# Carrying a linear-attention state on every 64 tokens, in two visits a tile, instead of every 128

## What is computed

```python
def step(carry, inp):
    kv, ksum = carry
    kt, vt, qt = inp
    kv = kv + jnp.einsum('bhd,bhe->bhde', kt, vt)
    ksum = ksum + kt
    num = jnp.einsum('bhd,bhde->bhe', qt, kv)
    den = jnp.einsum('bhd,bhd->bh', qt, ksum)[..., None] + EPS
    return ((kv, ksum), num / den)
```

## Time and profile before

| | us |
|---|---|
| median of 3 runs | 1939.35 |
| lowest and highest | 1937.93 to 1939.39 |
| the profiled execution | 1939.27 |
| span of its trace | 1937.6 |
| PE busy | 1904.0 (98%) |
| DVE busy | 1586.2 (82%) |
| POOL busy | 891.4 (46%) |
| ACT busy | 664.3 (34%) |

### The profile page before, as it was taken

One profiled execution on the slowest core, in us unless ns is written; L12 is line 12 of the kernel. 1 busy time (PEld: TensorE's weight loads), 2 busy tenths in 40 slices (PEclk: granted clock), 3 DMA queues, 4 the chain that ended last, 5 costly groups with the idle time before them and its releaser, 6 DMA issues. The chain is left out here.

```text
span 1937.6 us, 60626 instructions
## 1 busy us (share of the span) xinstructions
PE 1904.0 (98%) x25412; PEld 1671.4 (86%) x25412; DVE 1586.2 (82%) x3379; ACT 664.3 (34%) x1297; POOL 891.4 (46%) x979
## 2 busy tenths in 40 slices
PE   7999999999999999999999999999999999999997
PEld 6788888888888888888888888888888888888886
DVE  6878878887879888778878987887788897878787
ACT  4333333333333233333333333333332333323331
POOL 4355443455443554534554445545345544355422
PEclk9999999999999999999999999999999999999998
DMA  6343234433343432333423334323433334333222
GB/s 202 94 133 106 92 111 125 127 110 104 100 127 110 128 118 74 127 121 115 122 99 105 116 111 138 113 85 111 132 116 116 98 96 129 113 126 119 75 72 84
DMA packets 171202, 218.03 MB, mean 113 GB/s; under 512 B 24369, under 2 KB 85809, under 8 KB 170929
## 3 DMA queue, kind: packets, MB, share of 16 engines
q1 hardware_dynamic: 168528, 213.59, 34.7%
q10 hardware_dynamic: 2400, 0.55, 0.1%
HBM read 151.02 MB, written 63.04 MB: 110 GB/s over the span
## 5 line engine op out<-in xcount | busy, mean ns | idle before, releaser
L1258 POOL TENSOR_TENSOR k_sum<-k_sum,q_raw 128x512 f32<-128x512 f32 x128 | 165.0, 1290 | 556.2 <-DVE q_raw L933 556.2
L836 ACT ACTIVATE e_tmp<-ring,bias_n 128x512 f32<-128x512 f32 x256 | 176.1, 688 | 509.9 <-PE ring L651 506.8
L922 DVE TENSOR_TENSOR s_mask<-ring,causal 128x512 f32<-128x512 f32 x512 | 314.9, 678 | 0.0
L669 PE MATMUL ring<-wv_hi,xt_hi 128*128 128x260 f32 x1024 | 299.3, 292 | 0.0
L669 PE MATMUL ring<-wo_hi,o_hi 128*128 128x260 f32 x1024 | 287.8, 282 | 1.2 <-ACT o_hi L886 1.0
L669 PE MATMUL ring<-wv_lo,xt_hi 128*128 128x260 f32 x1024 | 288.8, 282 | 0.0
L669 PE MATMUL ring<-wv_hi,xt_lo 128*128 128x260 f32 x1024 | 288.8, 282 | 0.0
L669 PE MATMUL ring<-wo_lo,o_hi 128*128 128x260 f32 x1024 | 288.4, 282 | 0.0
L669 PE MATMUL ring<-wo_hi,o_lo 128*128 128x260 f32 x1024 | 287.3, 284 | 0.9 <-DVE o_lo L1170 0.9
L886 ACT ACTIVATE o_hi<-num_ps 128x512 fp32r<-128x512 f32 x128 | 76.4, 597 | 475.0 <-PE num_ps L750 474.9
L651 PE MATMUL ring<-xt_hi,wk_hi 128*128 128x512 f32 x512 | 207.9, 406 | 5.2 <-DVE xt_lo L998 3.2
(11 more groups left out here) (140 smaller groups left out, 4060.3 us busy)
## 6 DMA issues: line engine op xcount, KB each, us to landing
x_tok<-in_x SPq DMA_DIRECT2D x128, 256.0 KB, 3.7
res<-in_x SPq DMA_DIRECT2D x128, 256.0 KB, 2.8
out<-res SPq DMA_DIRECT2D x128, 256.0 KB, 2.1
x_in<-in_x_t SPq DMA_DIRECT2D x124, 256.0 KB, 4.6
keys_turned<-k_turned SPq DMA_DIRECT2D x112, 256.0 KB, 2.0
k_tok<-keys_turned SPq DMA_DIRECT2D x448, 64.0 KB, 2.0
x_rows<-moments_rows SPq DMA_DIRECT2D x31, 512.0 KB, 3.7
k_t<-in_wk_t SPq DMA_DIRECT2D x4, 256.0 KB, 8.3
```

Source lines behind the costliest of these rows:

```text
L669: mm = pe.matmul(bank[:, 0:HW], rows[a](k), w[b][:, k, h, :], start=n == 0, stop=n == 3 * KD - 1)
L836: act.activation(e_tmp[:, m], bank, ACT.Relu, bias=bias_n[:, m, g:g + 1], scale=-1.0).then_inc(phi_relu.handle, 1)
L922: dve.tensor_tensor(s_mask[:, j], ring[:, st.bank(u)].rearrange("p (g t) -> p g t", g=KD), repeat(causal, KD), ALU.mult).then_inc(free[st. ...
L1258: pool.tensor_tensor(k_sum[:, g], k_sum[:, g], q_raw[:, g], ALU.mult).then_inc(prod.handle, 1)
```

## The change

A tile is now cut into two halves of 64 tokens (`HT`, `s` = 0 and 1), and the state is carried on after each half.

- **Scores** are computed only inside a half: 64 by 64 for each head and half. The two halves of the keys go to the two halves of the partitions of the same bank, so a bank now holds 256 columns. There are 32 products a tile in place of 16, on parts of 32 rows by 64 columns. The mask and `s_mask` are half as large, and so is each masking instruction of VectorE.
- **The state** is multiplied with the queries of each half (`from_state`, 16 products with 64 columns, twice a tile), and `add_state` adds the keys and values of each half (contraction over 64 rows, 16 products, twice a tile). The two halves use columns in different banks of `num_ps`. `sum_state` on VectorE and `keep_state` on ScalarE run twice a tile.
- **Two visits.** The first half's state work (`early_half`: `from_state` and `add_state`) is done at the end of the tile before, behind its output projection O; the second half's (`late_half`) stands where the state work stood.
- **Values in two goes.** The masked scores times values is done in `from_own_rows`, heads of the first bank on rows 0 to 63 and of the second bank on rows 64 to 127, and, behind the scores of the next tile (in tile 2 behind the denominators), in `from_other_rows` with the banks crossed. So no two row halves write one bank at a time. ScalarE's `o_hi` waits for the second go.
- The last tile of a sequence needs its keys too now, because its first half feeds its second; there are 128 turns of keys where there were 112. The first `early_half` of a block's tile 0 also waits for the values of tile 0.

The core of the diff:

```diff
-    KEY_TILES = [(b, c) for b in range(n_blocks) for c in range(TPB) if b % 2 == 0 or c < TPB - 1]
+    KEY_TILES = [(b, c) for b in range(n_blocks) for c in range(TPB)]
...
-    kv_ps = num_ps[:, 0, 2 * P:2 * P + KD * HD]
+    kv_ps = [num_ps[:, n, 2 * P:2 * P + KD * HD] for n in range(2)]
...
             for g in range(KD):
                 if c == 0:
                     pe.wait_ge(free[BANK[("R", g)]].handle, st.freed(("R", g)))
-                for j, u in enumerate(scores_of(c)):
-                    rows = slice(j * HD, (j + 1) * HD)
-                    mm = pe.matmul(ring[:, st.bank(u), g * P:(g + 1) * P], k_t[rows, par, g, t], q_div[rows, par, g, t],
-                                   start=True, stop=True, skip_group_check=True, tile_position=(j * HD, 0))
+                for s in range(2):
+                    t = slice(c * P + s * HT, c * P + (s + 1) * HT)
+                    for j, u in enumerate(scores_of(c)):
+                        rows = slice(j * HD, (j + 1) * HD)
+                        mm = pe.matmul(ring[s * HT:(s + 1) * HT, st.bank(u), g * HT:(g + 1) * HT],
+                                       k_t[rows, par, g, t], q_div[rows, par, g, t], start=True, stop=True,
+                                       skip_group_check=True, tile_position=(j * HD, s * HT))
...
+        def from_state(off, c, s):
...
+            pe.wait_ge(kv_kept.handle, kv_kept.at(HPG * n))
+            begins = (0, 1) if s == 0 else (1,) if first_of_pair(off, c, 0) else ()
             for g, j in HEADS_OF_PASSES:
+                r = j // 2
+                rows, t = slice(r * HT, (r + 1) * HT), slice(c * P + s * HT, c * P + (s + 1) * HT)
+                out, col = num_at(g, j, s)
+                pe.matmul(out, kv_diag[rows, g, j * HD:(j + 1) * HD], q_div[rows, off % 2, g, t],
+                          start=r in begins and g < 2, stop=r != s, skip_group_check=True, tile_position=(r * HT, col))
+
+        def add_state(off, c, s):
...
+            n = KEY_TILES.index((off, c))
+            pe.wait_ge(keys_in[n % 2].handle, 16 * HPG * (n // 2 + 1))
+            rows = slice(s * HT, (s + 1) * HT)
...
+        def products(c, crossed, done):
+
+            for four in range(0, HEADS, HPG):
+                r = four // HPG % 2
+                s = 1 - r if crossed else r
+                rows = slice(s * HT, (s + 1) * HT)
+                for g, j in HEADS_OF_PASSES[four:four + HPG]:
+                    head = (g * HPG + j) * HD
+                    out, col = num_at(g, j, s)
+                    mm = pe.matmul(out, v_tok[rows, c, head:head + HD], s_mask[rows, j, g], start=False, stop=True,
+                                   skip_group_check=True, tile_position=(s * HT, col))
+                if four >= HEADS // 2:
+                    mm.then_inc(done.handle, 1)
...
+        def from_other_rows(st, c):
+
+            pe.wait_ge(own_summed.handle, own_summed.at(2 * st.lin(TPB, st.off, c + 1)))
+            products(c, True, summed)
+
+        def early_half(st, off, c):
+
+            pe.wait_ge(o_lo.handle, o_lo.at(TPB * off + c))
+            if c == 0:
+                before = st if off > st.off else st.prev
+                for h in range(2):
+                    u = ("V", (0, h))
+                    pe.wait_ge(free[BANK[u]].handle, before.freed(u))
+            from_state(off, c, 0)
+            add_state(off, c, 0)
...
                 if attn:
-                    from_state(st, c)
-                    add_state(st, c)
-                    from_tile(st, c)
+                    late_half(st, c)
...
                     two_halves(st, "O", c, [lambda k, h=h: o_t[h][:, k, :] for h in range(2)], w_o)
+                    if not st.alone():
+                        early_half(st, *tile_after(st.off, c))
                 if c == 2 and proj:
                     spread_reciprocals(st)
...
                 if attn:
                     residual(st, c)
+                    if proj:
+                        sum_state(*tile_after(st.off, c), 0)
```

More of the change, by code:

```diff
@@ L18 @@
 KD = D // P
+HT = P // 2
 HPG = P // HD
@@ L727, in from_state @@
-        def from_state(st, c):
-            pe.wait_ge(o_lo.handle, o_lo.at(st.lin(TPB, st.off, c)))
-            if first_tile(st, c):
+                for s in range(2):
+                    t = slice(c * P + s * HT, c * P + (s + 1) * HT)
[4 more added lines that the diff above has]
+                                       skip_group_check=True, tile_position=(j * HD, s * HT))
+                        if g == KD - 1 and s == 1:
+                            mm.then_inc(full[st.bank(u)].handle, 1)
@@ L740, in from_tile @@
-        def from_tile(st, c):
+                r = j // 2
[4 more added lines that the diff above has]
+        def add_state(off, c, s):
+            if last_of_pair(off, c, s):
+                return
+            n = KEY_TILES.index((off, c))
+            pe.wait_ge(keys_in[n % 2].handle, 16 * HPG * (n // 2 + 1))
+            rows = slice(s * HT, (s + 1) * HT)
+            for g in range(KD):
+                for j in range(HPG):
+                    cols = slice((g * HPG + j) * HD, (g * HPG + j + 1) * HD)
+                    mm = pe.matmul(kv_ps[s][j * HD:(j + 1) * HD, g * HD:(g + 1) * HD], k_tok[rows, n % 2, j, g],
+                                   v_tok[rows, c, cols], start=first_of_pair(off, c, s) and g == 0, stop=True,
+                                   skip_group_check=True, tile_position=(s * HT, j * HD))
+            if s == 0:
+                mm.then_inc(kv_added.handle, 1)
@@ L746, in from_tile, with late_half @@
                     pe.wait_ge(free[BANK[u]].handle, st.before(BANK[u]) + CREDIT)
[L747 to L765 removed]
+            products(c, False, own_summed)
+        def from_other_rows(st, c):
[10 more added lines that the diff above has]
+            add_state(off, c, 0)
+        def late_half(st, c):
+            if c == 0:
+                for k in banks_of("V"):
+                    pe.wait_ge(free[k].handle, free[k].at(st.before(k)))
+            from_state(st.off, c, 1)
+            add_state(st.off, c, 1)
+            from_own_rows(st, c)
         def body(st):
@@ L780, in body @@
                         pe.wait_ge(xt_lo.handle, xt_lo.at(TPB * (st.off + 1)))
-                    chunks(st, c, 0, 1)
-                if attn:
-                    if c == 0 and st.off == 0:
-                        pe.wait_ge(ready["wo_t"].handle, READY["wo_t"])
-                    if c == 0:
-                        for k in banks_of("V"):
-                            pe.wait_ge(free[k].handle, free[k].at(st.before(k)))
-                    from_state(st, c)
-                    add_state(st, c)
-                    from_tile(st, c)
+                    chunks(st, c, 0)
+                    if attn and starts_late(st.off, c):
+                        pe.wait_ge(ready["wo_t"].handle, READY["wo_t"])
+                        early_half(st, st.off, c)
+                    chunks(st, c, 1)
+                if attn:
+                    late_half(st, c)
                 if c == 1 and not attn:
@@ L800, in body @@
                     scores(st, st.off + 1, 0)
+                if attn and (c != 2 or not proj):
+                    from_other_rows(st, c)
                 if proj:
@@ L805, in body @@
                 if attn:
+                    if st.alone() and not last:
+                        early_half(st, st.off, c + 1)
                     if st.alone():
@@ L871, in body @@
                 last = c == TPB - 1
+                if attn and not starts_late(st.off, c):
+                    keep_state(st.off, c, 0)
                 if c == 0 and proj:
@@ L1154, in body @@
                 if proj:
-                    chunks(st, c, 0, 1)
+                    chunks(st, c, 0)
+                    if attn and starts_late(st.off, c):
+                        sum_state(st.off, c, 0)
+                    chunks(st, c, 1)
                 if c == 0 and not attn:
@@ L1202, in body @@
                     choose(4, range(13, 17))
+                if st.alone() and not last:
+                    sum_state(st.off, c + 1, 0)
                 if attn:
                     residual(st, c)
+                    if proj:
+                        sum_state(*tile_after(st.off, c), 0)
                     if c != 2 or not proj:
```

125 lines of the change are left out of this document (58 added, 67 removed).

## The result

The changed kernel takes **2204.31 us** in the median (2191.31 to 2207.82, 4 runs), the kernel before 1939.37 us beside it (1937.93 to 1942.03): a ratio of 1.135, with a 95% interval from 1.130 to 1.140. The direction was forecast, the size was not: +265 us where +15 stood, far outside 1931 to 1990. The profiled execution has a span of 2206.1 us.

What follows compares the result with a forecast made beforehand. TensorE's own stream, busy 98% of the span, was taken as the bound. 1939.3 - 17 (stages) + 28 and 5 (keys) + 2 (masked bank) - 5 (shorter masks) + 2 (last block) = 1954 us, range 1931 to 1990.

Steps and rivals of the forecast that it cites:

- rival 4: TensorE's small stages: instructions come too slowly, 0.1 us a tile, +10 us, 1964 us; joint chance with the forecast 0.62.
- My stage sum: TensorE's stages if it never waits: 3.11 us a tile for 3.27, with three corrections -17 us.
- Scores: Scores stage on TensorE: 64 records in 8 turns of 64 columns, 0.68 us a tile.
- Add: State update of one half on TensorE: 0.36 us as before, since a half fills only four parts.
- The state half: State of one half times the queries on TensorE: 4 turns of 64 columns, 0.27 us.
- a go with the values: One of two goes of masked scores times values on TensorE: 0.38 us, twice a tile.
- rival 3: Row halves don't share the array: scores take 16 turns, 1996 us, over 2050 if other stages suffer; chance 0.13.
- Keys: TensorE's adds wait for keys through DRAM: +28 us at the next block's tile 0, +5 at tile 3.
- kv_diag: Later halves of tiles 1 to 3 need ScalarE's copies, which end before the chunks do: wait 0.
- VectorE: Sign of being right: VectorE busy about 110 us less, with a mask's mean near 420 ns.

Runs made afterwards that it cites:

- values doubled: The kernel before, with each product of values issued as two products of 64 columns; 1969.85 us, ratio 1.016.
- state alone in halves: The changed kernel with whole-tile scores and one go of whole-tile values, only the state read and added to in two halves; 2064.87 us, ratio 1.064.
- scores and values alone in halves: The kernel before with scores and values in the changed form, state once a tile, products between halves left out; 2022.55 us, ratio 1.044.
- scores and values doubled: The kernel before, with each scores and each values product issued as two products of 64 columns; 2120.59 us, ratio 1.093.
- whole scores: The changed kernel with scores computed for whole tiles again, 16 products for 32, and two mask instructions a bank; 2138.31 us, ratio 1.105.
- values in quarters: The kernel before, with each product of values issued as four products of 32 columns; 2222.29 us, ratio 1.145.
- The holds: The kernel before, with TensorE made to wait once a block for extra ScalarE copies: seven copies 2080.72 us, ratio 1.072; five copies 2013.95 us, ratio 1.038.

## Why the prediction was right or wrong

| kernel | small records a tile | us | issue waits | us at half clock |
|---|---|---|---|---|
| before | 256 | 1939 | 0.7 | 11 |
| values doubled | 320 | 1970 | 11 | 13 |
| state alone in halves | 384, two places | 2065 | 0.5 | 33 |
| scores and values alone in halves | 384 | 2023 | 87 | 89 |
| scores and values doubled | 384 | 2121 | 32 | 49 |
| whole scores | 448, two places | 2138 | 28 | 62 |
| values in quarters | 448 | 2222 | 161 | 173 |
| changed kernel | 512, two places | 2204 | 115 | 178 |

**The step that failed is rival 4.** I named it, instructions that "don't come fast enough", and priced it at 0.1 us a tile, 10 us. No row stood behind that price. I had read that 32 records take 0.36 us, and asked whether TensorE can run them, not where they come from. The trace of before had the row that speaks of it, the q8 queue with 203 packets, and the arithmetic was open: 256 small records in a row in about 3.1 us before, 384 in about 2.4 us after. Measured, it is 114 us more in issue waits, and some 75 to 84 us for half clock behind these and the other waits (75 where the stretches in idle time are left out).

The clock was in no term of mine at all, although rival 4 as well as every wait that I did forecast should have carried it. The holds show its price.

That the direction came out proves little. The +15 of my sum came from waits, the keys above all, with stages that got cheaper. Measured, the keys' wait is 21 of the 265 us, and the stages got dearer.

The Trainium skill, "Runtime: NRT & Kernel Launch", section "Instruction fetch mechanics", says that instructions are fetched in order, in blocks of 16 KiB or 256 instructions. That agrees with q8's 16 KB packets and with breaks at one fixed place in 256. For the size of the memory it gives two figures: 128 KiB, 2048 instructions, for TensorE, and two lines of 16 KiB. In the changed kernel no page began to move more than 3.9 us before the page ahead of it began to run, which fits the two lines and not eight. It also says that the fetch is hidden behind the time that each instruction takes to issue. That does not hold here: 65 breaks lie at a page's edge.

**The accounts.** The two traces lie 268.5 us apart (2206.1 and 1937.6): 114 (issue) + 30 (other waits: 59.1 for 29.6) + 75 (clock, outside idle time) + the rest, some 50, in the stages and in pauses too short to be listed. My stage sum was -17. Two terms were mis-sized:
- Scores: 0.68 forecast, 0.84 measured, +0.16 x 128 = 20 us. Behind the first, the turns stand 0.058 us apart, about as in my sum (0.054), but from the 28th record to the last the products come 25 ns apart on average.
- Add: 0.36 to 0.37 forecast, 0.50 and 0.47 measured, together about +0.24 a tile, 30 us. From first to last record 0.34 in place of 0.26: a half on parts of 64 rows is slower than a whole on parts of 128.

-17 + 20 + 30 = +33; the remaining 17 or so of that rest I can't place. The state half (0.27) and a go with the values (0.38 forecast, 0.39 measured) were right, and so was the claim that row halves share the array: rival 3 did not happen.

**Keys.** Forecast 28 us at tile 0's early add and 5 at tile 3's, measured 17.0 and 4.4, 21.4 in 24 waits of over 0.15 us. The mechanism was right, and worth little.

**kv_diag** I had at 0; it is 13.4 us in 5 waits, one at the start and four in the last 60 us, where few chunks or none cover it. **VectorE** fell by 95 us (about 110 forecast), a mask takes 412 ns (near 420 forecast). Two slips of my sum hang on nothing: 0.68 less 0.42 over 512 masks is 133 us and not 137, and a half add is 0.36 in the list and 0.37 in the sum.

**The two halves of the change** cost 125 and 82 us alone and 265 together: 58 us more than their sum. A likely reason, not tested by itself, is that the cluster of 384 passes in 2.4 us when both are in and in 2.6 when only scores and values are. Neither pays: the first by its doubled stages, the second only by pages and clock. No kernel here beats the one before.

**What stays open.** Why a page with a break behind it begins to move only 1.6 us on average (eight in ten: 0.8 to 2.7) after the one ahead began to run; what sets the distance of 17 ns in the quarters and of 25 ns in the scores; and which holds of equal length bring half clock.

## What to carry to other kernels

Count instructions by the time in which they pass, not only by their number: where small products stand in a row, compare 256 records with the time that a page took to come (4.2 us here), before any price of the array is weighed. This is a warning and no limit: in the kernel before, 14 of 201 pages ran in under 4.2 us, the shortest in 3.3, without a break, and in the changed kernel 34 of 73. Put small stages in two places rather than one, where no other wait stands right behind them, and halve columns only where the record count does not rise with it. Price a wait on TensorE with the half clock that can follow: here 0.4 to 0.6 us on top of a stand-still of 1.7 us, 1.4 to 1.5 us on top of one of 3.1 us.

## What the runs showed of the hardware

- TensorE's instructions come in packets of 16 KB, 256 records; in the changed kernel a page with a break behind it needed 1.2 us on the way, and 1.4 us more until its first record ran.
- In nine kernels nearly all breaks with the releaser "issue" (11 to 87 a kernel, 415 of 419 in all) lie at the same number modulo 256.
- A stand-still of TensorE that only a semaphore caused brought the clock to half in 20 of 31 cases at 3.06 us and in 6 of 31 at 1.74 us, for 3.4 or 6.8 us.
- On parts of 32 rows and 128 weight columns, 64 moving columns take as long a turn as 128 (0.11 us); on parts of 128 rows and 32 weight columns, a values stage of twice the products with 64 columns takes 1.03 us for 1.01.
- In no stage did products of 32 to 64 columns come closer than 15 ns on average; the longest such run, 64 products of 32 columns, kept 17.
